# Half of a depthwise convolution moved into the projection stage, three small projections made serial, and weight sums redistributed

## The reference

```python
xn = layernorm(x)
# branch s (DT_RANK = 6, D_STATE = 16, Din = 96)
u   = layer_norm(xn, ln_w, ln_b) @ in_proj_W.T          # 2048 x 96
u   = silu(conv1d_depthwise(u, conv_w, width 3) + conv_b)
dbc = u @ x_proj_W.T                                    # 6 + 16 + 16 columns
delta = softplus(dbc[:, :6] @ dt_proj_W.T + dt_proj_b) * 0.001
state[t] = exp(delta*A) * state[t-1] + delta*Bp*u       # for 16 states
y   = sum over states of state*Cp + u*D_param
s   = y @ out_proj_W.T + xn
# gate: quantized linears, weight scale = 1 / mean(|w|)
h = silu(bitlinear(xn, w1)) * bitlinear(xn, w3)         # hidden 5632
g = silu(bitlinear(h, w2))
out = x + s * g
```

## Time and profile before

| | us |
|---|---|
| median of 2 runs (3558.9 and 3616.24) | 3587.57 |
| the profiled execution: time | 3561.62 |
| its slowest core, first to last instruction | 3560.1 |
| its fastest core | 3534.7 |
| TensorE busy on the slowest core | 2507.3 |
| VectorE busy | 1863.1 |
| ScalarE busy | 1649.7 |
| GpSimd busy | 152.1 |

### The profile page before, as it was taken

How to read it: one execution, slowest core, us unless ns; L and a number is a source line. 1 busy time by engine, 2 the same in 40 slices (tenths; PEclk the granted TensorE clock), 3 DMA queues, 4 the chain that set the end, 5 groups by cost and what they waited for, 6 DMA issues and landing times. The chain is left out here.

```text
span 3560.1 us, 29270 instructions; the slowest of 8 cores (3534.7 to 3560.1 us)
## 1 busy us (share of the span) xinstructions
PE 2507.3 (70%) x9525; PEld 1091.4 (31%) x9525; DVE 1863.1 (52%) x1805; ACT 1649.7 (46%) x1343; POOL 152.1 (4%) x283
## 2 busy tenths in 40 slices
PE   2454554997999999999999992464655734767773
PEld 1222221333444444444444441121222311323321
DVE  3545444884444444444444454464544644555654
ACT  3353615884666666666666651534353221111111
POOL 0000001110000000000000000000000000000000
PEclk9999996557999999999999995787878866888875
DMA  3222204984444444444444422646455234332213
GB/s 113 83 94 84 72 11 161 333 296 142 142 141 143 141 143 141 144 140 144 138 143 141 146 83 77 189 130 182 122 163 143 77 123 142 120 111 101 83 59 130
DMA packets 92610, 469.13 MB, mean 132 GB/s; under 512 B 12924, under 2 KB 13004, under 8 KB 58060
## 3 DMA queue, kind: packets, MB, share of 16 engines
q1 hardware_dynamic: 54412, 282.69, 23.7%
q0 software_dynamic: 38048, 184.57, 15.3%
HBM read 381.20 MB, written 85.98 MB: 131 GB/s over the span
## 5 line engine op out<-in xcount | busy, mean ns | idle before, releaser
L1506 PE MATMUL ps_f<-w2s,qhs 128*128 128x512 bf16 x2816 | 686.1, 410 | 422.7 <-DVE f_half L1525 275.3
L1065 PE MATMUL ps_a<-qx,w1q 128*128 128x512 bf16 x2816 | 628.5, 382 | 85.7 <-DVE hbuf L1110 73.8
L1073 PE MATMUL ps_b<-qx,w3q 128*128 128x512 bf16 x2816 | 622.1, 379 | 0.0
L1506 PEld LDWEIGHTS ps_f<-w2s,qhs 128*128 128x128 bf16 x2816 | 290.5, 104 | 819.9 <-issue 608.8
L1525 DVE TENSOR_TENSOR f_half<-f_half,ps_f 128x1024 f32<-128x1024 f32 x320 | 390.8, 1221 | 205.2 <-PE ps_f L1506 199.4
L1065 PEld LDWEIGHTS ps_a<-qx,w1q 128*128 128x128 bf16 x2816 | 274.0, 98 | 432.3 <-issue 113.6
L1073 PEld LDWEIGHTS ps_b<-qx,w3q 128*128 128x128 bf16 x2816 | 275.5, 98 | 332.3
L1404 ACT ACT_TABLE_LOAD x44 | 56.5, 1283 | 585.5 <-DVE fscr L1386 584.1
L1098 ACT ACT_TABLE_LOAD x88 | 112.9, 1283 | 444.9 <-DVE fscr L1089 444.9
L1386 DVE TENSOR_TENSOR fscr<-hbuf,shB 128x1024 int32<-128x1024 f32 x88 | 107.8, 1226 | 263.8 <-DMA hbuf<-h_scr 250.2
L1106 DVE TENSOR_TENSOR fscr<-ps_b,sxinvB 128x1024 f32<-128x1024 f32 x88 | 107.8, 1225 | 231.8 <-ACT fscr L1098 231.8
(11 more groups left out here) (197 smaller groups left out, 2907.9 us busy)
## 6 DMA issues: line engine op xcount, KB each, us to landing
wstg<-w1L SPq DMA_DIRECT2D x44, 1024.0 KB, 8.8
wstg<-w3L SPq DMA_DIRECT2D x44, 1024.0 KB, 11.2
w2m<-w2T SPq DMA_DIRECT2D x88, 512.0 KB, 5.0
h_scr<-hbuf POOLq DMA_DIRECT2D x88, 512.0 KB, 4.1
hbuf<-h_scr POOLq DMA_DIRECT2D x88, 512.0 KB, 5.8
wstg<-w2T SPq DMA_DIRECT2D x30, 1024.0 KB, 8.8
wstg<-w1L POOLq DMA_DIRECT2D x22, 1024.0 KB, 7.2
wmst<-w1L POOLq DMA_DIRECT2D x22, 1024.0 KB, 7.5
```

Source lines behind the costliest of these rows:

```text
L1065: t.matmul(ps_a[pu][:, j * 512:(j + 1) * 512], w1q[par][:, cc * 128:(cc + 1) * 128], qx[:, cc * L + th * HALF + j * 512: cc * L + th * HAL ...
L1073: inst = t.matmul(ps_b[pu][:, j * 512:(j + 1) * 512], w3q[par][:, cc * 128:(cc + 1) * 128], qx[:, cc * L + th * HALF + j * 512: cc * L + t ...
L1506: inst = t.matmul(ps_f[pu][:, j * 512:(j + 1) * 512], qhs[sp][:, k * HALF + tt * 128: k * HALF + (tt + 1) * 128], w2s[sp][:, k * C + ch * ...
```

## The change

`ucv` is allocated earlier, so that it exists in ph01, and `ipcorr` becomes a part of the scratch tile `fscr1`. Weight sums in ph01 go from three units in rounds 1 to 7 to two units in rounds 2 to 7. After round 5, whose tokens 0 to 1279 have gone through the tail up to block 4, ph01 does the convolution, Silu and the u*D term for the columns 0 to 1023. In attn, the convolution, Silu and u*D are done for columns 1024 to 2047 only. The three projections there all write PSUM partitions from 0, and each waits for the copy of the one before it. The counts of weight sums in attn (four, eight, four in each step) are the same in the text of the program; how many steps have them follows from what ph01 leaves.

```diff
--- before.py
+++ after.py
@@ -132,6 +132,7 @@
 
     es_xin = ExitStack()
     xin = es_xin.enter_context(nc.sbuf_tensor("xin", [D, L], F32))
+    ucv = es_xin.enter_context(nc.sbuf_tensor("ucv", [D, L], F32))
     wmst = [wstg[0], wstg[1]] + \
         [es_xin.enter_context(nc.sbuf_tensor(f"wmst{i}", [128, NCC * 128],
                                              F32)) for i in range(2)]
@@ -150,8 +151,8 @@
     sxB = SBp("sxB", (128, ET))
     r2B = SBp("r2B", (D, ET))
     rm2B = SBp("rm2B", (D, ET))
-    ipcorr = SBp("ipcorr", (D, ET))
     bvec = SBp("bvec", (D, 2))
+    ipcorr = fscr1[0:D, ET:2 * ET]
 
     ps_es = ExitStack()
     PS1 = lambda n, shp: ps_es.enter_context(nc.psum_tensor(n, list(shp), F32))
@@ -677,11 +678,11 @@
                 v.wait_ge(s_t.h, ipd_hist[e])
                 v.tensor_tensor(fscr1[0:D, 0:ET], ps_ip[:], r2B[:], ALU.mult)
                 v.drain()
-                v.tensor_scalar(ipcorr[:], rm2B[:], bvec[:, 1:2],
+                v.tensor_scalar(ipcorr, rm2B[:], bvec[:, 1:2],
                                 bvec[:, 0:1], ALU.mult, ALU.subtract)
                 v.drain()
                 s_v.inc(v.tensor_tensor(xin[:, e * ET:(e + 1) * ET],
-                                        fscr1[0:D, 0:ET], ipcorr[:],
+                                        fscr1[0:D, 0:ET], ipcorr,
                                         ALU.subtract))
                 v.drain()
             evac_hist[e] = s_v.v
@@ -697,8 +698,43 @@
                 emit_xdma(e + 2)
             if e + 1 < NE:
                 emit_head(e + 1)
-            if e >= 1:
-                emit_means(blk, 3, "scalar")
+            if e >= 2:
+                emit_means(blk, 2, "scalar")
+            if e == 5:
+                @blk.vector
+                def _(v):
+                    v.wait_ge(s_v.h, evac_hist[4])
+                    v.tensor_scalar(ucv[:, 0:HALF], xin[:, 0:HALF],
+                                    convw_sb[:, 1:2], convb_sb[:],
+                                    ALU.mult, ALU.add)
+                    v.drain()
+                    v.scalar_tensor_tensor(ucv[:, 1:HALF],
+                                           xin[:, 0:HALF - 1],
+                                           convw_sb[:, 0:1], ucv[:, 1:HALF],
+                                           ALU.mult, ALU.add)
+                    v.drain()
+                    s_v.inc(v.scalar_tensor_tensor(
+                        ucv[:, 0:HALF], xin[:, 1:HALF + 1],
+                        convw_sb[:, 2:3], ucv[:, 0:HALF],
+                        ALU.mult, ALU.add))
+                    v.drain()
+                cvA = s_v.v
+
+                @blk.scalar
+                def _(sc):
+                    sc.wait_ge(s_v.h, cvA)
+                    s_a.inc(sc.activation(ucv[:, 0:HALF], ucv[:, 0:HALF],
+                                          AF.Silu))
+                    sc.drain()
+                silA = s_a.v
+
+                @blk.vector
+                def _(v):
+                    v.wait_ge(s_a.h, silA)
+                    s_v.inc(v.scalar_tensor_tensor(
+                        y_sb[:, 0:HALF], ucv[:, 0:HALF], Dp_sb[:],
+                        y_sb[:, 0:HALF], ALU.mult, ALU.add))
+                    v.drain()
         emit_tail(NE - 1)
 
     ps_es.close()
@@ -711,7 +747,6 @@
     es_sc = ExitStack()
     SBs = lambda n, shp, dt=F32: es_sc.enter_context(nc.sbuf_tensor(n, list(shp), dt))
     sel = SBs("sel", (NST, NST * D))
-    ucv = SBs("ucv", (D, L))
     bp_sb = SBs("bp_sb", (NST, L))
     cp_sb = SBs("cp_sb", (NST, L))
     delta = SBs("delta", (D, L))
@@ -741,20 +776,18 @@
         @blk.vector
         def _(v):
             v.wait_ge(s_v.h, xin_ok)
-            s_v.inc(v.tensor_scalar(ucv[:], xin[:], convw_sb[:, 1:2],
-                                    convb_sb[:], ALU.mult, ALU.add))
-            v.drain()
-        c1d = s_v.v
-
-        @blk.vector
-        def _(v):
-            v.wait_ge(s_v.h, c1d)
-            v.scalar_tensor_tensor(ucv[:, 1:L], xin[:, 0:L - 1],
-                                   convw_sb[:, 0:1], ucv[:, 1:L],
+            v.tensor_scalar(ucv[:, HALF:L], xin[:, HALF:L],
+                            convw_sb[:, 1:2], convb_sb[:],
+                            ALU.mult, ALU.add)
+            v.drain()
+            v.scalar_tensor_tensor(ucv[:, HALF:L], xin[:, HALF - 1:L - 1],
+                                   convw_sb[:, 0:1], ucv[:, HALF:L],
                                    ALU.mult, ALU.add)
             v.drain()
-            s_v.inc(v.scalar_tensor_tensor(ucv[:, 0:L - 1], xin[:, 1:L],
-                                           convw_sb[:, 2:3], ucv[:, 0:L - 1],
+            s_v.inc(v.scalar_tensor_tensor(ucv[:, HALF:L - 1],
+                                           xin[:, HALF + 1:L],
+                                           convw_sb[:, 2:3],
+                                           ucv[:, HALF:L - 1],
                                            ALU.mult, ALU.add))
             v.drain()
         cvd = s_v.v
@@ -762,39 +795,39 @@
         @blk.scalar
         def _(sc):
             sc.wait_ge(s_v.h, cvd)
-            s_a.inc(sc.activation(ucv[:], ucv[:], AF.Silu))
+            s_a.inc(sc.activation(ucv[:, HALF:L], ucv[:, HALF:L], AF.Silu))
             sc.drain()
         ud = s_a.v
         emit_means(blk, 4, "scalar")
 
-        @blk.tensor
-        def _(t):
-            t.wait_ge(s_a.h, ud)
-            inst = None
-            for si, (c0, w, off) in enumerate(((0, RK, 0), (RK, NST, 32),
-                                               (RK + NST, NST, 64))):
+        xp_ev = {}
+        for si, (c0, w, dst) in enumerate(((0, RK, dbc_dr),
+                                           (RK, NST, bp_sb),
+                                           (RK + NST, NST, cp_sb))):
+            @blk.tensor
+            def _(t):
+                t.wait_ge(s_a.h, ud)
+                if si > 0:
+                    t.wait_ge(s_v.h, xp_ev[si - 1])
+                inst = None
                 for j in range(4):
-                    inst = t.matmul(ps_sc[off:off + w, j * 512:(j + 1) * 512],
+                    inst = t.matmul(ps_sc[0:w, j * 512:(j + 1) * 512],
                                     xprojT_sb[:, c0:c0 + w],
                                     ucv[:, j * 512:(j + 1) * 512],
                                     start=True, stop=True)
-            s_t.inc(inst)
-        mmd = s_t.v
-
-        @blk.vector
-        def _(v):
-            v.wait_ge(s_t.h, mmd)
-            v.tensor_copy(dbc_dr[0:RK, :], ps_sc[0:RK, :])
-            v.drain()
-            v.tensor_copy(bp_sb[0:NST, :], ps_sc[32:32 + NST, :])
-            v.drain()
-            s_v.inc(v.tensor_copy(cp_sb[0:NST, :], ps_sc[64:64 + NST, :]))
-            v.drain()
-        xp_done = s_v.v
+                s_t.inc(inst)
+            mmd = s_t.v
+
+            @blk.vector
+            def _(v):
+                v.wait_ge(s_t.h, mmd)
+                s_v.inc(v.tensor_copy(dst[0:w, :], ps_sc[0:w, :]))
+                v.drain()
+            xp_ev[si] = s_v.v
 
         @blk.tensor
         def _(t):
-            t.wait_ge(s_v.h, xp_done)
+            t.wait_ge(s_v.h, xp_ev[2])
             inst = None
             for j in range(4):
                 inst = t.matmul(ps_sc[0:D, j * 512:(j + 1) * 512], dtT_sb[:],
@@ -846,7 +879,8 @@
             v.wait_ge(s_a.h, dltd)
             v.tensor_tensor(du[:], delta[:], ucv[:], ALU.mult)
             v.drain()
-            s_v.inc(v.scalar_tensor_tensor(y_sb[:], ucv[:], Dp_sb[:], y_sb[:],
+            s_v.inc(v.scalar_tensor_tensor(y_sb[:, HALF:L], ucv[:, HALF:L],
+                                           Dp_sb[:], y_sb[:, HALF:L],
                                            ALU.mult, ALU.add))
             v.drain()
         dud = s_v.v
```

## The result

The changed kernel takes 3588.9 us (median of 42 runs) and the kernel before 3566.7 us (41 runs measured beside it): a ratio of 1.0063, with an interval of 1.0047 to 1.0079. It is 22 us slower, and the measurement tells that from zero with ease. Some executions of either kernel are disturbed; they are in the medians, but the ratios leave them out.

What follows compares the result with a forecast made beforehand. First stage: TensorE and VectorE hand work to and fro; scan: TensorE full at clock 0.50. Terms 0 + 7.6 - 2.7 - 0.85 + 11.6 - 1.07 + 9.85 = +24.4 us, 3561.6 to 3586 us; range 3563 to 3625.

Steps and rivals of the forecast that it cites:

- Fewer weight sums in the first stage: First stage: nine units leave it, all hidden ahead of ScalarE's idle stretch; gain 0, bounds 0 and 0.
- The insert: Half convolution, Silu and y update after round 5, in a VectorE chain without slack; +7.6 us.
- The feared 8.9: Upper bound in us for the work inserted after round 5, if the write shifted by one column is slow by itself.
- ScalarE's late statistics: Block 6: statistics kept back by ScalarE's wait for the convolution, ready near 449; hidden, with 25 us of cover.
- The convolution left in attn: Second block: VectorE's part halves, GpSimd's iota and comparison do not shrink; -2.7 us.
- Silu and y update: Ahead of projections and scan: halved Silu 1.91 to 1.06, -0.85 us; halved y update 2.35 to 1.28, -1.07 us.
- The projections: Before the scan: three serial groups of 7.11 us, each with hand-over and copy, 28.9 us against 17.3; +11.6 us.
- its rival (+4.6): Projections: second and third group spaced 0.43 us; loss 4.6, or 1.1 if all three; chance 0.22.
- Four sums behind the scan: Scan's end: the set of step 15 begins when the scan has ended, uncovered; +9.85 us.
- Scan steps, the clock, the loads: Scan: steps stay 13.65 us at clock 0.50; rivals full clock, 27 us saved, and weight loads binding, chance 0.05 each.
- the no-change case: Whole kernel: measured time within about 2% of the kernel before; chance 0.92, against faster 0.03 and slower 0.05.
- the rival at 3559 us: Scan gets the full clock: ScalarE sets steps of 11.85 us, 27 us saved; chance 0.05.

Runs made afterwards that it cites:

- sums_only: The kernel before with only the weight sums redistributed, two units in rounds 2 to 7 of the first stage; 3580.5 us, ratio 1.0013.
- sums_in_rounds: The kernel before with ten weight sums in place of three in each of rounds 1 to 7; 3573.2 us, ratio 0.9999.
- scan_128rows: The kernel before with the scan matmuls' operands over 128 rows, those behind the sixteenth zero; 3522.7 us, ratio 0.9894.
- combined_again: Against the kernel before: convolution pieces in VectorE's waits, projections at three offsets without waits, three sums a round, 128 rows in the scan; 3516.0 us, ratio 0.9881.

## Why the prediction was right, and where it was wrong

**Fewer weight sums in the first stage, 0.** Right, and for the reason given: `sums_only` has rounds of the same length, and 497.8 us to the first y update of the scan as before. The term was bounded by "0 and 0"; for taking sums away that holds. In the other direction there is a price (`sums_in_rounds`, 3 to 9 us over the cores for seven more in each of seven rounds), which the prediction did not need.

**The insert, +7.6.** Right to 0.1 us (7.50), each operation at the length that was scaled from the rows of other sizes: 0.81, 1.28, 1.28, 1.28 + 1.06, 1.28. The feared 8.9 did not come: the shifted write L711 took 1.28 us. ScalarE's late statistics stayed hidden: the next round takes 61.4 us, and its 0.3 us over the 61.1 of before are one late start of VectorE (0.42 us of "issue" ahead of a copy to `xcol`), a cost that the sum does not have.

**The convolution left in attn, -2.7.** Right (-2.68). The step that mattered was to read L744 and L752 as VectorE and GpSimd taking turns, so that GpSimd's part does not shrink with the columns. `scan_128rows` shows where the contention ends. There VectorE's two-input operation at 542.93 ran beside GpSimd's zero filling and iota, which write and don't read, and took its plain 2.35 us. (The one-input operation ahead of it did not come off so: beside the zero filling it took 2.77 us, where 1.35 is its size's duration.) The Trainium skill's page "SBUF — State Buffer", section "Who interferes with whom", says that a VectorE instruction with two SBUF inputs contends with a GpSimd instruction that reads SBUF and not with one that only writes; the traces agree for this form, 4.08 us beside the comparison against 2.35 for twice the columns beside the filling.

**Silu and y update, -0.85 and -1.07.** Right.

**The projections, +11.6.** This is the term that was mis-sized. The sign and the mechanism held, the size did not: +8.2. What failed in it is "3 x (7.11 + 0.10 + 2.28 + 0.14)", with 7.11 us for a group taken from L800. The groups took 5.39, 6.54 and 5.29 us. The hand-overs came as in the sum (2.28, and 2.53 us of idleness on TensorE). The prediction gave the two spacings, 0.85 and 0.43 us, and treated them as a choice for a whole group. The weight loads of the first group, in the timeline of after, have the time since the one before them in their starts:

```profile
560.25 0.13 PEld L814 LDWEIGHTS ps_sc<-ucv,xprojT_sb 96*6 96x6 f32 x1 [0.72 <-issue]
560.82 0.09 PEld L814 LDWEIGHTS ps_sc<-ucv,xprojT_sb 96*6 96x6 f32 x1 [0.44 <-issue]
561.25 0.09 PEld L814 LDWEIGHTS ps_sc<-ucv,xprojT_sb 96*6 96x6 f32 x1 [0.34 <-issue]
...
574.41 0.15 PEld L814 LDWEIGHTS ps_sc<-ucv,xprojT_sb 96*16 96x16 f32 x1 [0.44 <-issue]
575.27 0.15 PEld L814 LDWEIGHTS ps_sc<-ucv,xprojT_sb 96*16 96x16 f32 x1 [0.70 <-issue]
```

The idle time ahead of a load goes from 0.72 to 0.34 us: the spacing falls inside the first group, near its end. The second group keeps the long spacing; the third, from 573.85 on, begins with the short one, has the long one from 575.27 and falls back near its end. So the spacing changes inside the groups and between them, and the either-or for whole groups is what mis-sized the term: the forecast and its rival (+4.6) were each half right, and +8.2 lies between.

**Four sums behind the scan, +9.85.** Right (+9.8), on the whole chip.

**Scan steps, the clock, the loads.** Right: the step is 13.65 us and the clock 0.50 in the scan, and the fourth set of sums did not stretch it.

**The chances.** This is the step that failed most. The prediction said "2% is about what a measurement of this kernel tells from no change" and gave the no-change case 0.92, while its own sum said +0.7% and all but one of its terms were known to within a microsecond or two. What it had to go by were two runs, 57 us apart, and that distance between two single executions is not the error of a comparison of many. The comparison's interval is 0.16% to either side with some forty runs of each, and 0.2 to 0.4% with ten to thirteen. Within 2% the outcome is the one forecast as likely; as a statement on whether the change costs anything, it was wrong. The sum should have been carried to the end: its low end, +10 us (0.28%), is already above 0.16%, so a small loss deserved most of the chance. The range is not worked out to its ends either: 3588 and 29 make 3617 and not 3625, and the rival at 3559 us lies below 3563.

**Still open.** Why a VectorE instruction starts 0.35 us late now and then. When TensorE's spacing changes inside a group: over the 8 cores the projections differ by up to 1.3 us, and this was only averaged. In the first group the windows print a clock of 1.00 while the spacing is the long one, so this column does not settle it. What part of the slowest core's time is due to which core it is.

## What to carry to other kernels

Moving work forward to an engine that is idle "on average" pays only if it stands in that engine's queue where it waits anyway: half of the convolution with Silu and the y update cost 7.5 us in one piece behind the broadcast copies, and 0.3 us when its parts stood in two waits of VectorE. Work that balances a later stage must be counted out to its last unit: taking 9 hidden units from the first stage left four behind the last scan step, fully exposed. And a small sum that is well founded is a forecast of sign: compare it with the interval that repeated comparison gives, not with the spread of two runs.

## What was not expected of the hardware

- **TensorE full and at 0.50.** In the scan it was busy for 85 of 85 us and for 100 of 100 us at the 1.2 GHz level with operands of 16 rows, and with 128 rows, most of them zero, it was granted 0.86 to 0.91 at 58 to 69% busy. The Trainium skill's page "TensorE: Matmul & The Clock Gate", section "Why this matters for your kernels", advises continuous work to reach the full clock; for 16 rows these traces don't bear that out. What in the rows the chip responds to is not shown by these runs: only their number was changed, and the added ones hold zeros.
- **Small copies beside large loads.** A two-row copy of SyncE on which TensorE waits landed about 3 us later (5.90 for 2.84 us) while 1 MB loads ran at a DMA share of 0.63.
- **A gap can cost spacing too.** In the projections eight records took 5.3 and 6.5 us behind gaps of 2.5 us and 3.6 us without a gap ahead.
- **Late starts.** A few VectorE instructions in each kernel start 0.35 us late with no wait that the profile shows, and work put into the queue ahead of them moves the place. In the middle of a scan paced by TensorE that cost nothing, in its last step 0.35 us. In `combined_again`, paced by VectorE, two steps take 12.2 us instead of 11.8, and nothing makes up for it.
